# One recurrence step: the second operand of a scan is copied from PSUM to SBUF by ScalarE

## The reference

```python
def step(state, inp):
    qt, kt, vt, bt = inp
    kk = kt[..., :, None] * kt[..., None, :]
    bb = bt[..., None, None]
    state = state * (1.0 - bb * kk) + bb * (vt[..., :, None] * kt[..., None, :])
    out_t = jnp.einsum('bhij,bhj->bhi', state, qt)
    return (state, out_t)
```

## Time and profile before

| what | value |
|---|---|
| device time, median of 2 runs | 871.97 us (870.27 to 873.67) |
| the profiled execution: its own time | 872.05 us |
| the profiled execution: span from first to last instruction | 870.3 us |
| share of the span busy: PE, DVE, POOL, ACT | 82%, 69%, 51%, 41% |
| recurrence, first scan's start to last readout's end | 209.3 us to 590.1 us |
| mean granted TensorE clock | 0.918 of full speed |

### The profile page before, as it was taken

How to read it: one execution, slowest core, us unless ns; L and a number is a source line. 1 busy time by engine, 2 the same in 40 slices (tenths; PEclk the granted TensorE clock), 3 DMA queues, 4 the chain that set the end, 5 groups by cost and what they waited for, 6 DMA issues and landing times. The chain is left out here.

```text
span 870.3 us, 20449 instructions
## 1 busy us (share of the span) xinstructions
PE 713.8 (82%) x7740; PEld 481.8 (55%) x7740; DVE 602.0 (69%) x857; ACT 353.0 (41%) x561; POOL 446.8 (51%) x249
## 2 busy tenths in 40 slices
PE   3577769886999999999999999985899769977774
PEld 3365534445777777777777777764677423322231
DVE  3578738888999999999999999992577521000014
ACT  2356624443455555455554444543455321210000
POOL 1579600003999999999999999992112100000000
PEclk9789989998999999999999999996999959868775
DMA  5100000000001010000000000003920279999977
GB/s 112 49 2 0 1 1 0 0 0 14 8 14 38 14 36 12 6 12 12 12 12 9 9 12 12 14 14 83 404 59 2 74 313 374 418 413 421 413 318 248
DMA packets 49212, 86.34 MB, mean 99 GB/s; under 512 B 5553, under 2 KB 32753, under 8 KB 49169
## 3 DMA queue, kind: packets, MB, share of 16 engines
q1 hardware_dynamic: 45616, 83.33, 26.2%
q10 hardware_dynamic: 3552, 2.43, 0.9%
HBM read 76.31 MB, written 9.44 MB: 99 GB/s over the span
## 5 line engine op out<-in xcount | busy, mean ns | idle before, releaser
L896 POOL TENSOR_TENSOR read<-state,q_pos 128x1024 f32<-128x1024 f32 x128 | 300.4, 2365 | 28.7 <-DVE state L1005 22.4
L1005 DVE TENSOR_TENSOR_SCAN state<-fac,ps_up 128x1024 f32<-128x1024 f32 x128 | 290.0, 2277 | 8.6 <-ACT fac L940 8.6
L940 ACT ACTIVATE fac<-ps_xf 128x1016 f32<-128x1016 f32 x128 | 130.2, 1018 | 176.3 <-PE ps_xf L1039 159.9
L1039 PEld LDWEIGHTS ps_xf<-hot,xtab 64*128 64x128 f32 x2048 | 125.4, 188 | 58.0 <-ACT fac L940 43.8
L1039 PE MATMUL ps_xf<-hot,xtab 64*128 64x128 f32 x2048 | 148.4, 284 | 11.0 <-ACT fac L940 8.9
L1039 PE MATMUL ps_up<-hot,utab 64*128 64x128 f32 x2048 | 139.9, 276 | 19.5 <-DVE state L1005 19.5
L1039 PEld LDWEIGHTS ps_up<-hot,utab 64*128 64x128 f32 x2048 | 126.4, 189 | 25.1 <-issue 17.8
L905 POOL TENSOR_TENSOR utab<-tab 128x1024 f32 (+1 forms) x32 | 64.5, 2015 | 94.5 <-SPq L85 94.5
L1084 PE MATMUL ps_o<-read,sel 128*32 128x256 f32 x1024 | 82.7, 395 | 3.7 <-POOL read L896 3.7
L1635 DVE COPY h_t<-ps_ht 128x512 f32<-128x512 f32 x16 | 10.5, 687 | 79.9 <-PE ps_ht L1664 79.8
L995 DVE TENSOR_TENSOR xtab<-tab,ps_k 128x1024 f32<-128x1024 f32 x64 | 59.5, 929 | 1.5 <-PE ps_k L1031 1.5
(11 more groups left out here) (200 smaller groups left out, 981.9 us busy)
## 6 DMA issues: line engine op xcount, KB each, us to landing
w_sb<-in_L_ffn_w SPq DMA_DIRECT2D x32, 2048.0 KB, 20.1
rec_out<-osb SPq DMA_DIRECT2D x128, 32.0 KB, 1.5
ao<-rec_out SPq DMA_DIRECT2D x8, 512.0 KB, 4.1
out_dram<-h SPq DMA_DIRECT2D x8, 256.0 KB, 2.5
out_dram<-h ACTq DMA_DIRECT2D x8, 256.0 KB, 3.1
tok<-in_x SPq DMA_DIRECT2D x2, 512.0 KB, 10.8
exp_out<-eo SPq DMA_DIRECT2D x8, 128.0 KB, 18.5
oq<-exp_out SPq DMA_DIRECT2D x8, 128.0 KB, 3.0
```

The costliest lines, as they stand in the source:

```text
L896: nc.gpsimd.tensor_tensor(read[n % 2][:], state[n % 4][:].rearrange("p (b i t) -> p b i t", b=2, i=IB), q_pos[x.s][:, :, x.k].unsqueeze(2) ...
L940: nc.scalar.activation(fac[n % 2][:].rearrange("p (n t) -> p n t", t=T)[:, :, 1:], ps_x[:].rearrange("p (n t) -> p n t", t=T)[:, :, 1:], A ...
L1005: nc.vector.tensor_tensor_scan(state[n % 4][:], fac[n % 2][:], ps_u[n % 2][:], 0.0, ALU.mult, ALU.add)\
L1039: last = nc.tensor.matmul(dst[:, b * 512 + col * T:b * 512 + (col + 1) * T], stationary[rows], pos[rows], start=True, stop=True)
```

## The change

The update terms take one step more: after PE has written them to `ps_u[n % 2]`, ACT copies them to a new tile `upd[n % 2]` in SBUF, and the scan reads `upd` in place of `ps_u`. The two buffers of `upd`, 1024 floats each, lie in the storage of `w_all`. On ACT the copy of a unit stands right behind its `factors`, ahead of `outputs`, `mirror` and the next unit's work; it waits for PE's updates (`u_mm`) and for the scan two units back (`sc_ok`), which read the same buffer. The scan waits for the copy (`uc_ok`) in place of `u_mm`, and PE's `updates` waits for the copy two units back in place of the scan two units back.

The stages' chain semaphores are merged to one for VectorE (`vch`) and one for GpSimd (`pch`), with running counts; the links and waits themselves stay.

```diff
-        m = {"start": start}
+        m = {"start": start, "vch": Chain(nc.vector, sem("v_chain")), "pch": Chain(nc.gpsimd, sem("p_chain"))}
...
     fac = [sb(f"fac{i}", [P, UT]) for i in range(2)]
+    upd = [m["w_all"][:].rearrange("p k n -> p (k n)")[:, i * UT:(i + 1) * UT] for i in range(2)]
     state = [sb(f"state{i}", [P, UT]) for i in range(4)]
...
+            def updates(i, n):
+                x = Unit(i, n)
+                act.wait_ge(u_mm, START + x.u + 1)
+                act.wait_ge(sc_ok, START + x.u - 1)
+                nc.scalar.copy(upd[n % 2], ps_u[n % 2][:]).then_inc(uc_ok, 1)
+
...
                             queries(i, n + 1)
                         factors(i, n + 1)
+                        updates(i, n + 1)
                     if n % 4 == 1 and not (first and n == 1):
...
             factors(0, 0)
+            updates(0, 0)
             queries(0, 0)
...
-            ch = Chain(dve, sem("v_chain4"))
+            ch = m["vch"]
...
                 dve.wait_ge(a_ok, START + x.u + 1)
-                dve.wait_ge(u_mm, START + x.u + 1)
+                dve.wait_ge(uc_ok, START + x.u + 1)
                 dve.wait_ge(rd_ok, START + x.u - 3)
-                nc.vector.tensor_tensor_scan(state[n % 4][:], fac[n % 2][:], ps_u[n % 2][:], 0.0, ALU.mult, ALU.add)\
+                nc.vector.tensor_tensor_scan(state[n % 4][:], fac[n % 2][:], upd[n % 2], 0.0, ALU.mult, ALU.add)\
                     .then_inc(sc_ok, 1)
...
-                pe.wait_ge(sc_ok, START + x.u - 1)
+                pe.wait_ge(uc_ok, START + x.u - 1)
                 for ii in range(IB):
```

More of the change, by code:

```diff
@@ L197, in token_attention @@
         s_mm, e_tp, c_dg, c_mm, c1_ok, ln_ok = (sem(n) for n in ("s_mm", "e_tp", "c_dg", "c_mm", "c1_ok", "ln_ok"))
-        vch = sem("v_chain0")
         @block.sync
@@ L247, in _ @@
         def _(pool):
-            pch = Chain(pool, sem("p_chain0"))
+            pch = m["pch"]
             pch.link(nc.gpsimd.memset(ident[:], 0.0))
@@ L276, in _ @@
         def _(dve):
-            ch = Chain(dve, vch)
+            ch = m["vch"]
             dve.wait_ge(ld_e, START + 32)
@@ L455, in _ @@
         def _(dve):
-            ch = Chain(dve, sem("v_chain1"))
+            ch = m["vch"]
             def softmax_input(i, s):
@@ L641, in _ @@
         def _(dve):
-            ch = Chain(dve, sem("v_chain3"))
+            ch = m["vch"]
             mean_r, var_r = mean_row[:], var_row[:]
@@ L854, in recurrence @@
         block = ctx.enter_context(nc.Block())
-        (k_ok, st_ok, q_mm, q_ok, x_mm, u_mm, a_ok, t_dve, t_pool, t_act, sc_ok, rd_ok, sm_ok, oe_ok) = (
-            sem(n) for n in ("rk_ok", "rst_ok", "rq_mm", "rq_ok", "rx_mm", "ru_mm", "ra_ok", "rt_dve", "rt_pool",
+        (k_ok, st_ok, q_mm, q_ok, x_mm, u_mm, a_ok, uc_ok, t_dve, t_pool, t_act, sc_ok, rd_ok, sm_ok, oe_ok) = (
+            sem(n) for n in ("rk_ok", "rst_ok", "rq_mm", "rq_ok", "rx_mm", "ru_mm", "ra_ok", "ruc_ok", "rt_dve", "rt_pool",
                              "rt_act", "rsc_ok", "rrd_ok", "rsm_ok", "roe_ok"))
@@ L1181, in recurrent_outputs @@
         m["w1_ld"], m["w2_ld"], m["wbias"] = w1_ld, w2_ld, wbias
-        pch, ch = Chain(nc.gpsimd, sem("p_chain1")), Chain(nc.vector, sem("v_chain5"))
+        pch, ch = m["pch"], m["vch"]
         def each_step(tail, work):
```

## The result

The changed kernel takes 1102.11 us (median of 2 runs, 1100.35 to 1103.87) against 871.97 before: 1.267 times as long, 95% interval 1.263 to 1.271. Its profiled execution spans 1098.6 us, 228.3 us more than before.

The account below looks back on a forecast made before the run. DVE paces the recurrence, POOL having hardly more room. Full exclusion plus hand-overs makes four units 21.18 us, x 32 = 678 us against 380.8: +297 on 872.05 gives 1169 us; range 940 to 1220, about 8 in 10.

Parts of the forecast that it names:

- What bounds the kernel: Recurrence stage, 380.8 us: DVE paces it with 12.16 us of work per four units; POOL, 11.48, has hardly more room.
- exclusion: Recurrence: a two-SBUF scan and a POOL instruction cannot run at once; +297 us, 1169 us, own range 1103 to 1215; 72%.
- The scan's own duration: DVE's scan with both inputs in SBUF: 0.5 to 3.7 us slower over 128 scans, taken as 2 us.
- The saving of 65 ns: DVE's scan, by the skill's fixed costs: 62 cycles less from SBUF, 8 us in all, giving about 864 us.
- piecewise sharing: Rival, scan beside POOL in the recurrence: read path given out element by element; +124 us, 996 us (940 to 1060); 10%.
- the hand-over: From a scan's end on DVE to POOL's readout start: 0.15 us, four times in four units, making 20.58 into 21.18 us.
- The lower bound: DVE and POOL in the recurrence: only streaming parts exclude, fixed 151 and 175 ns taken off; 19.1 us per four units, 1103 us.
- a clock priced too low: PE's clock in the stretched stage: taken as nothing, 30 us added to the upper end; sign: 1.2 GHz, DVE waiting for ACT and PE.
- The copy on ACT: 128 copies of 128x1024 from PSUM on ACT: 1.03 us each, ACT about 33.8 us busy of 40, below the limit.
- the openings: 16 openings in the recurrence: ACT's copies cost DVE 0 to 1.25 us each, 0 to 20 us in all, 6 taken.
- No contention: Rival, scan beside POOL in the recurrence: second SBUF operand has its own path; 880 us, from 872.5 to 896; 15%.
- a gain: Rival, DVE's scan: it loses more than 0.14 us, giving 17 us; about 850 us; 3%.

Follow-up runs that it names:

- the split scan: The changed kernel with every scan issued as two instructions of 512 elements, the second releasing the readout: 1132.1 us, 1.301 times the kernel before.
- the memset: The changed kernel with POOL's readout replaced by a memset of the same tile, which reads nothing: 897.2 us, 1.031 times the kernel before.
- the copy-only run: The changed kernel with ACT's copy kept, but the scan reading PSUM and PE waiting for the scan again: 886.0 us, 1.020 times the kernel before.

## Why the prediction was right, and where it was off

**What bounds the kernel.** Right: DVE and POOL, nearly equally, with no room for one to wait for the other. That is why exclusion showed at once in the time.

**The scan's own duration.** I took 2 us for all scans, from rows that put the two-SBUF form of tensor_tensor 4 to 29 ns above the other. Measured: medians of 2278 against 2279 ns, nothing. The saving of 65 ns a scan, an estimate that I had worked out from the Trainium skill, "VectorE: DVE Perf Modes", section on the errata of SBUF-source operations, did not show either.

**The exclusion.** Right in mechanism, and right in that the value lay near full exclusion rather than at piecewise sharing: the two groups of readouts with none between, the rows in turn, and the split scan say that it holds for a whole instruction. The runs agree with what the Trainium skill says in "SBUF — State Buffer", section "Who interferes with whom", down to the memset: a POOL instruction that only writes is left alone.

**The size.** The step that was off is the hand-over, a term of the sum. I added 0.15 us for each scan (21.18 us for four units); the stage took 612.3 / 32 = 19.13 us. Two things were wrong in it. First, the 0.15 us is the way of a semaphore from DVE to POOL, and it lies on the path only if POOL is waiting for that scan. In the changed kernel POOL is behind, its next instruction stands ready, and it is idle for 12.8 us in all, of which 10.5 are before its first readout. Second, the next instruction gets through 0.1 to 0.2 us before the row in front ends, so that a scan and a readout together cost 4.29 us, not 2.28 + 2.37 = 4.65. Those 2.05 us in four units are 66 us, the whole distance from 1169 to 1102. The lower bound that I had worked out, exclusion of the streaming parts only, gave 19.1 us and 1103, and the result lies just below the 1103 to 1215 us that I gave to exclusion. That bound took off 0.33 us for a scan and a readout together, and the rows show 4.65 - 4.29 = 0.36; that the overlap is those fixed parts is not shown.

**What is late next.** I had DVE standing at its next scan all the time. In fact DVE was idle for 83.9 us before its scans. The waits of 210 to 800 us (total us, times, longest) and the timeline ahead of the scan of 500.56 show why:

```profile
PEld ps_o L1092 <- POOL read L896: 177.5, 61, 5.8
PE ps_o L1092 <- POOL read L896: 161.9, 46, 5.6
DVE state L1013 <- issue: 60.5, 27, 2.7
...
DVE state L1013 <- ACT w_all L948: 19.1, 11, 2.8
...
494.62 1.08 PE L1092 MATMUL ps_o<-read,sel 128*32 128x256 f32 x8 [5.62 <-POOL read L896]
495.63 2.08 PE L1047 MATMUL ps_xf<-hot,xtab 64*128 64x128 f32 x16
499.46 1.01 ACT L948 COPY w_all<-ps_up 128x1024 f32<-128x1024 f32 x1 [0.69 <-PE ps_up L1047]
```

PE's `sums` wait for late readouts, and PE's factors and updates of the next units stand behind them; so ACT, then DVE, are late too. The wait that the view puts down to "issue" ends as ACT's copy does: at 500.47, and the scan starts at 500.56. This costs nothing by itself, since POOL runs its undisturbed readouts in that time, and its rows fill the stage. The granted clock of 0.84 is in the same place: after PE had stood still for 5.62 us, its 16 matmuls of the factors took 2.08 us, at a granted clock of 0.50 (1.2 GHz). My comparison of busy shares in the earlier trace rows did not carry: PE was busy 28.83 of the 40 us from 400 us on, a larger share than the 57% that had run at 1.00. So the sign that I had named for a clock priced too low, DVE waiting for ACT and PE, did appear. The price of nothing held all the same: after its first readout POOL is idle for only 2.3 us in the whole stage.

**The copy on ACT.** 1.03 us estimated, 1.011 measured. For the openings I gave 0 to 20 us and took 6, "because ACT mostly runs ahead in the seven other units". The copy alone cost 16 us. The reason that I gave was beside the point: at the opening shown ACT was ahead, idle for 1.67 us until PE's factors came, but the copy stands between ACT's factors and the scan, and each of the 15 openings behind the first pays about one copy. That run has PE waiting for the scan again, so the 0.81 us that I took back per opening is not in it. In the changed kernel the price is hidden, and no run shows it there without contention.

**The rivals.** No contention would have come close to what the copy-only run shows (886 us; I had 880), but for that wait of PE; piecewise sharing (996) fell by the durations, since no readout lies between 2.45 and 4.2 us; a gain had no basis, since the scan's duration does not depend on where its second operand lies.

## What to carry to other kernels

Before an operand of a VectorE instruction is moved from PSUM to SBUF, look at what GpSimd runs beside it: if the instruction then has both inputs in SBUF and GpSimd reads SBUF, the two can take turns. Here, with a scan beside GpSimd's two-operand tensor_tensor, each scan cost GpSimd 1.93 us; no other VectorE instruction with two SBUF inputs was run beside it. The trace of before can't show this when no such pair overlaps in it; that absence is itself worth looking for, and a range should then reach to the sum of both engines' work. And an engine that shows 100% busy with fewer instructions than before may be standing still inside its rows: compare an instruction's duration with its undisturbed one.

## What the hardware showed that I had not expected

The exclusion is not free of overlap: counted back by its undisturbed duration, the instruction that waited starts about 0.2 us before the row of a scan ends, and a scan of 2.28 us holds a readout up by 1.98 us. And the two-SBUF scan costs DVE nothing by itself: 2278 ns in the median beside POOL's memsets, against 2279 ns from PSUM.
